# Two heads per strip in the value product, and an output chain that runs once per two batches

## What is computed

```python
def _mha(x, ctx, mask, qw, qb, kw, kb, vw, vb):          # H = 16 heads, D = 128
    q = _split_heads(x @ qw + qb); k = _split_heads(ctx @ kw + kb); v = _split_heads(ctx @ vw + vb)
    scores = jnp.einsum('bqhd,bkhd->bhqk', q, k) / np.sqrt(D // H) (+ mask)
    probs = jax.nn.softmax(scores, axis=-1)
    return jnp.einsum('bhqk,bkhd->bqhd', probs, v).reshape(...)
def _self_output(h, residual, w, b, g, be):
    h = h @ w + b + residual
    return (h - mean) * rsqrt(var + 1e-05) * g + be
ca = _mha(x, ctx, mask, cq.., ck.., cv..);  x = _self_output(ca, x, co_w, co_b, co_g, co_be)
sa = _mha(x, x, None, sq.., sk.., sv..);    x = _self_output(sa, x, so_w, so_b, so_g, so_be)
inter = gelu(x @ fi_w + fi_b);              x = _self_output(inter, x, fo_w, fo_b, fo_g, fo_be)
```

## Time and profile before

| | |
|---|---|
| median of 3 runs | 1085.51 us (1085.27 to 1091.91) |
| span of the profiled execution | 1077.5 us |
| PE busy | 966.2 us (90%) |
| PE weight loads | 747.5 us (69%) |
| DVE busy | 642.9 us (60%) |
| ACT busy | 571.7 us (53%) |
| POOL busy | 468.3 us (43%) |
| exponentials of the 128 chunks, starts | 35.0 to 432.3 us |
| mean granted TensorE clock | 0.975 of full speed |

### The profile page before, as it was taken

How to read it: one execution, slowest core, us unless ns; L and a number is a source line. 1 busy time by engine, 2 the same in 40 slices (tenths; PEclk the granted TensorE clock), 3 DMA queues, 4 the chain that set the end, 5 groups by cost and what they waited for, 6 DMA issues and landing times. The chain is left out here.

```text
span 1077.5 us, 23011 instructions
## 1 busy us (share of the span) xinstructions
PE 966.2 (90%) x8722; PEld 747.5 (69%) x8726; DVE 642.9 (60%) x2007; ACT 571.7 (53%) x1209; POOL 468.3 (43%) x752
## 2 busy tenths in 40 slices
PE   4889998998999799988989999888888999999998
PEld 2556666565656566777877887766667777778787
DVE  3657777677778564665763333446888457466241
ACT  4768887777676465423334332123333845755553
POOL 6246675758686744665520000233445244213010
PEclk9989999999999899999999999989999999999999
DMA  7756443323332120000002331300000331521421
GB/s 179 188 137 163 114 122 80 85 72 105 84 99 70 41 84 7 15 12 6 6 26 67 108 108 54 111 20 15 20 21 11 92 100 25 94 80 40 138 65 53
DMA packets 72942, 78.56 MB, mean 73 GB/s; under 512 B 8469, under 2 KB 64132, under 8 KB 72832
## 3 DMA queue, kind: packets, MB, share of 16 engines
q1 hardware_dynamic: 67104, 69.61, 23.2%
q0 software_dynamic: 4096, 6.84, 3.0%
q10 hardware_dynamic: 1632, 0.64, 0.3%
HBM read 38.25 MB, written 11.68 MB: 46 GB/s over the span
## 5 line engine op out<-in xcount | busy, mean ns | idle before, releaser
L1286 DVE TENSOR_REDUCE arena<-pb 128x8 f32<-128x1024 f32 (+1 forms) x128 | 128.4, 1007 | 60.0 <-PE pb L647 56.5
L1780 ACT ACTIVATE arena<-pb 128x1024 f32<-128x1024 f32 (+1 forms) x128 | 130.8, 1022 | 58.9 <-PE pb L663 51.0
L2292 POOL DMA_INDIRECT arena<-yd,arena x64 | 63.9, 999 | 141.4 <-issue 141.3
L1834 ACT ACTIVATE arena<-pb 128x256 f32<-128x256 f32 x128 | 48.0, 383 | 131.0 <-PE pb L832 103.6
L831 PE MATMUL pb<-XLT,arena 128*128 128x256 f32 x256 | 80.2, 396 | 10.0 <-DVE arena L1445 7.5
L680 PE MATMUL pb<-arena 77*32 77x128 f32 (+1 forms) x2048 | 85.1, 285 | 0.0
L2171 POOL DMA_INDIRECT xd<-XB,arena x64 | 64.0, 1000 | 33.1 <-issue 19.2
L832 PE MATMUL pb<-XLT,arena 128*128 128x256 f32 x256 | 78.0, 387 | 0.0
L2030 ACT ACTIVATE arena<-pb,arena 128x264 f32<-128x264 f32 x128 | 54.7, 482 | 37.4 <-PE pb L1135 37.3
L2088 POOL TENSOR_SCALAR arena<-arena 128x4 f32<-128x4 f32 x48 | 9.4, 196 | 147.2 <-DVE arena L1241 144.8
L1441 DVE SCALAR_TENSOR_TENSOR arena<-arena,pb 128x256 f32<-128x256 f32 x128 | 53.0, 414 | 25.5 <-ACT arena L1834 19.7
(11 more groups left out here) (233 smaller groups left out, 2386.1 us busy)
## 6 DMA issues: line engine op xcount, KB each, us to landing
arena<-arena SPq DMA_DIRECT2D x190, 128.0 KB, 2.4
arena<-in_pe SPq DMA_DIRECT2D x32, 514.5 KB, 3.7
arena<-in_pr SPq DMA_DIRECT2D x8, 768.0 KB, 5.0
arena<-arena SPq DMA_DIRECT2D x43, 77.0 KB, 2.2
xd<-arena SPq DMA_DIRECT2D x8, 320.0 KB, 3.0
arena<-xd SPq DMA_DIRECT2D x8, 320.0 KB, 5.7
yd<-arena SPq DMA_DIRECT2D x8, 320.0 KB, 5.2
XO<-in_x SPq DMA_DIRECT2D x8, 256.0 KB, 3.2
```

What stands on the lines that cost most here:

```text
L1286: e.tensor_reduce(NM[i % 2][0][:, b, 4 * h:4 * h + 4, :].rearrange("p t h -> p h t"), sc, AX, ALU.max, negate=True).then_inc(v_max, 1)
L1780: e.activation(PT[n % 2][0:nk, :], bk2[1][0:nk, :], ACT.Exp, scale=SC8).then_inc(a_exp, 1)
L2292: e.indirect_dma_start(G[x % 8], None, yd, bass.IndirectOffsetOnAxis(ap=IDG.bitcast(U32)[:, k, b:b + 1], axis=0), bounds_check=None, oob_i ...
```

## The change

V gets 18 columns a head (eight of V, one of ones, nine of zeros), in two tiles of its own (`VA`) instead of in the three sets. The two heads of a pair now share a strip: the first head's weights are its 18 columns and what follows; the second's begin nine columns ahead of its own, so that its nine land in places 9 to 17 of the strip, and its matmul accumulates onto the first. A bank then holds two batches, and the chain behind it runs once per pair of batches: `out_sums`, `ttr`, `on`, `to`, `ont`, `two`, `tw` at beats 4, 5, 6, 6, 6, 7, 8 and four beats later for the second pair, with one buffer of each tile instead of two. With only two `VA` tiles, `values` moves from beat -14 to -8 and `va` from -13 to -7, and values get a semaphore of their own.

The bias of V is added in `ont`'s copy (a bias column instead of a plain copy). so_b and fo_b are added once to the shift rows of the layer norm ahead (`join_rows` on POOL), and taken off again in the copies of the turned groups (`turned_less`), so the eight additions for s units and the eight for the feed-forward go; for c units POOL still adds co_b. The four small products at the start go.

```diff
@@ pe @@
-                if h == 0:
+                if j % 4 == 0:
                     L.wait_ge(a_va, i + 1)
                     L.wait_ge(*free[4])
-                    free[4] = (a_os, 4 * i + b + 1)
+                    free[4] = (a_os, 2 * i + b // 2 + 1)
                 L.wait_ge(a_exp, n + 1)
-                for q in (2 * h, 2 * h + 1):
+                c = 128 * (2 * (b % 2) + h)
+                for half in range(2):
                     for k in range(4):
-                        h9, t, h2 = 144 * b + 9 * (4 * q + k), 2 * (q - 2 * h) + k // 2, k % 2
-                        ins = e.matmul(bk[4][32 * k:32 * k + 32, 128 * q:128 * q + 128], va[0:nk, h9:h9 + 32],
-                                       PT[n % 2][0:nk, 512 * h2 + 128 * t:512 * h2 + 128 * t + 128],
-                                       start=True, stop=True)
+                        v0 = VW * (NH * b + 8 * h + 2 * k + half) - 9 * half
+                        p0 = 512 * half + 128 * k
+                        ins = e.matmul(bk[4][32 * k:32 * k + 32, c:c + 128], va[0:nk, v0:v0 + 32],
+                                       PT[n % 2][0:nk, p0:p0 + 128], start=(half == 0), stop=(half == 1))
...
-                for i in at(n, -14, "c", lo=2):
-                    values(i)
-                for i in at(n, -14, "s", lo=2):
+                for i in at(n, -8, lo=2):
                     values(i)
@@ act @@
-                e.activation(OS[x % 2], bk[4], ACT.Copy).then_inc(a_os, 1)
+                e.activation(OS, bk[4], ACT.Copy).then_inc(a_os, 1)
...
-                L.wait_ge(p_kqv, 3 * i + 3)
+                L.wait_ge(p_val, i + 1)
                 L.wait_ge(g_vo, 1)
-                if i >= 3:
-                    L.wait_ge(p_pv, 8 * (i - 2))
+                if i >= 2:
+                    L.wait_ge(p_pv, 8 * (i - 1))
...
+            def turned_less(g, j, ready, done):
+
+                L.wait_ge(v_neg, 1)
+                L.wait_ge(*ready)
+                e.activation(xlt(g), bk[5], ACT.Identity, bias=NEGB[:, j:j + 1]).then_inc(done, 1)
...
-                e.activation(ONT[x % 2], bk[7][:, 0:128], ACT.Copy).then_inc(a_ont, 1)
+                e.activation(ONT, bk[7][:, 0:256], ACT.Identity, bias=vb[:, j:j + 1]).then_inc(a_ont, 1)
...
-                for i in at(n, -13, lo=2):
+                for i in at(n, -7, lo=2):
                     va(i)
@@ dve @@
+                L.tick(e.reciprocal(RC, v4[:, :, :, 8]))
+                L.own_done()
+                e.tensor_tensor(ON.rearrange("p (s h d) -> p s h d", h=2, d=8), v4[:, :, :, 0:8],
+                                RC.unsqueeze(3).to_broadcast([128, 16, 2, 8]), ALU.mult).then_inc(v_on, 1)
...
+                e.tensor_tensor(x2, bk[7][:, 0:256], x2, ALU.add).then_inc(v_tw, 1)
@@ pool @@
+            def join_rows():
+
+                L.wait_ge(d_rows, 32)
+                L.tick(e.tensor_tensor(R_["co_be"], R_["co_be"], R_["so_b"], ALU.add))
+                L.tick(e.tensor_tensor(R_["so_be"], R_["so_be"], R_["fo_b"], ALU.add))
...
-            def bias_ffn(g):
-                L.front_done()
-                L.wait_ge(p_tf, g + 1)
-                e.tensor_tensor(grp(XB, g), grp(XB, g), bcast(R_["fo_b"], GB), ALU.add).then_inc(g_fb, 1)
-                L.in_front(g_fb, g + 1)
...
-                for i in at(n, 2, "s"):
                     bias_out(i)
```

More of the change, by code:

```diff
@@ L95 @@
 NU = len(UNITS)
+VW = 18
 NCH = 8 * NU
@@ L134, in at, with pair_at @@
     return [i] if r == 0 and lo <= i < hi and UNITS[i][0] in kinds else []
-def block_at(n, d, kinds="cs"):
-    return [(i, b) for b in range(4) for i in at(n, d + 2 * b, kinds)]
+def pair_at(n, d, kinds="cs"):
+    return [(i, p) for p in range(2) for i in at(n, d + 4 * p, kinds)]
 def chunk_at(n, d):
@@ L373, in program @@
                 ("SC", (128, 512)), ("TG", (128, 512)))})
-        EWP = [rl(128, 1029) for _ in range(3)]
+        EWP = [rl(128, 1029) for _ in range(2)]
         XE, YT = r(128, 8, N8), r(128, 8, N8)
-        EWP.append(r(128, 1029))
+        EWP += [r(128, 1029) for _ in range(2)]
         OHP += [(r(128, 8, CAP2), r(128, 8, CAP2))]
@@ L755, in ttr, with to, two @@
                 for q in range(4):
-                    ins = e.transpose(bat(bk[5], q), OS[x % 2][:, 128 * q:128 * q + 128], ident)
+                    ins = e.transpose(bat(bk[5], q), bat(OS, q), ident)
                 ins.then_inc(p_ttr, 1)
                 free[5] = (v_on, x + 1)
-            def to(i, b):
-                x = 4 * i + b
+            def to(i, p):
+                x = 2 * i + p
                 L.wait_ge(v_on, x + 1)
                 L.wait_ge(*free[7])
-                e.transpose(bk[7][:, 0:128], ON[x % 2][1], ident).then_inc(p_to, 1)
+                for b in range(2):
+                    ins = e.transpose(bat(bk[7], b), bat(ON, b), ident)
+                ins.then_inc(p_to, 1)
                 free[7] = (a_ont, x + 1)
-            def two(i, b):
-                x = 4 * i + b
+            def two(i, p):
+                x = 2 * i + p
                 L.wait_ge(a_ont, x + 1)
                 L.wait_ge(*free[7])
-                e.matmul(bk[7][:, 0:128], ONT[x % 2], W[UNITS[i][0] + "o"], start=True, stop=True).then_inc(p_two, 1)
+                for b in range(2):
+                    ins = e.matmul(bat(bk[7], b), bat(ONT, b), W[UNITS[i][0] + "o"], start=True, stop=True)
+                ins.then_inc(p_two, 1)
                 free[7] = (v_tw, x + 1)
@@ L2129, in pool @@
             e.memset(mhalf, -0.5)
-            for s in range(3):
-                ins = e.memset(SETS[s][2], 1.0)
+            for s in range(2):
+                ins = e.memset(VA[s], 0.0)
+            L.tick(ins)
+            L.own_done()
+            for s in range(2):
+                ins = e.memset(VA[s][:, 0:GB * NH * VW].rearrange("p (h d) -> p h d", d=VW)[:, :, 8:9], 1.0)
             ins.then_inc(g_vo, 1)
```

234 lines of the change are left out of this document (92 added, 142 removed).

## The result

The changed kernel takes 1101.87 us (median of 17 runs, 1092.06 to 1110.55); the kernel before, run beside it, 1086.46. The ratio is 1.0111, 95% interval 1.0082 to 1.0140. Two repeats beside the experiments gave 1.0132 (1.0091 to 1.0173) and 1.0092 (1.0058 to 1.0126). So it is slower by about 12 us, just at the 1% that I had called measurable. (The two medians are 15.4 us apart; the ratio leaves out two of the 17 executions of the changed kernel, which fell into a slower state.) My forecast was +5 us. 1101.9 lies inside the range of 1072 to 1103, at its upper edge, but outside the 1080 to 1098 that the replay itself had claimed; the 12 us of the ratio, put onto the 1085.51 it started from, would be 1097.5, just inside that too.

What follows compares the result with a forecast made beforehand. The chain of second score product and exponential was taken to pace the quiet units, though TensorE looks full. Terms 6.5 + 5 - 2 - 3.5 - 1 = +5 gave 1077.5 + 5 + 8.0 = 1090.5 us, range 1072 to 1103.

Steps and rivals of the forecast that it cites:

- The replay of a quiet unit: Unit 3 beat by beat: values wait for ScalarE's query copies, beat 0 takes 4.55 us, unit +1.3; units 1 to 5 +6.5.
- The spread chain: Beat 5's first s1 waits for spread query operands (ScalarE, POOL, DMA), 1.65 us later, swallowing the 0.6 gained in beats 3 and 4.
- All of it shifts with s1, so the gains of beats 1 to 3 are swallowed: Units 7, 9, 11, 13: beat 0 +1.6, VectorE, POOL and ScalarE work behind s1 shifts too; 4 x 1.3 = +5 us.
- units 6, 8, 10 and 12: Values cost only +1.0 in beat 0, later beats give 0.7, 0.5 and 0.3: 4 x -0.5 = -2 us.
- rival B: New gaps in beats 0 and 5 pull TensorE's clock down; nine dips of 1.5 us make 1104 us; 18%.
- because VectorE waits in these beats: VectorE's strided reads in the attention beats: from nothing to some 10 us, taken as hidden and left unpriced.
- Head and tail: Head -1 us (unit 2's values leave unit 0, small bias products go); tail, units 14, 15 and after, -3.5 us (fewer transposes).
- 8.0 us lie around the span: Profiled span 1077.5 us against the runs' median 1085.51; 8.0 us added to the forecast span.
- POOL's relief: Eight plus eight bias additions removed from POOL, some 20 us, counted at nothing because POOL is waited for behind L1248.
- The bias column: ScalarE copies with a bias column cost at least 0.05 us more each, 2 us over 48 copies, mostly hidden.
- A: Freed time comes through on all engines: 1065 us, or about 1075 with half of the waits left; 22%.
- C: In the value product the second head's matmul waits for the first in its strip: 35 us, 1125 us; 2%.

Runs made afterwards that it cites:

- e1: Changed kernel with the value projection and its copy two beats later, so no longer behind fresh queries on bank 6: 1071.97 us, ratio 0.9937.
- e2: Kernel before with only the move of values and their copy, with a semaphore of their own; no packing, pairs or folded biases: 1100.47 us, ratio 1.0218.
- e3: Changed kernel with the value projection in the same place but written to bank 7, so without the wait: 1071.69 us, ratio 0.9930; again 1068.20 us, 0.9886.
- e6: e3 with 16 unread additions of 128x480 put back on POOL where the bias additions had stood: 1088.12 us, ratio 0.9999.
- e7: e3 with two transfers of the queries' middle part put ahead of the wait for POOL's low part in SyncE's queue: 1084.20 us, ratio 0.9964.
- e5: e3 with 32 unread blocks of four transposes put back on TensorE, in beats 3 and 7 of every unit: 1093.98 us, ratio 1.0069.
- e9: e3 with 32 unread copies of 128x480 put back on ScalarE behind the exponentials of beats 2 and 6: 1075.22 us, ratio 0.9960.
- e8: Changed kernel with five unread filling matmuls ahead of each value projection in beat 0 only: 1089.97 us, ratio 1.0088.
- e4: Changed kernel with unread filling matmuls, five ahead of each value projection (beat 0), three ahead of each unit's first score product (beat 5): 1088.47 us, ratio 1.0101.

## Why the prediction came out as it did

**The replay of a quiet unit was right.** Beat by beat in unit 3, forecast and found: 4.55 and 4.70, 1.95 and 1.78, 1.85 and 1.85, 1.56 and 1.77, 1.56 and 1.66; beats 5 to 7 together 7.8 and 7.4; the unit 19.2 and 19.1. The mechanism is shown from both sides by e1, e2 and e3: values behind fresh queries on one bank wait for ScalarE, and s1 and s2 wait behind them. Units 1 to 5 come to +6.8 for +6.5, though not unit by unit: unit 2 has 20.9 us for 18.2 in the two executions in which its clock was 0.92, and 19.5 in the one at full clock.

**The spread chain** as what swallows the gain of beats 3 and 4 was half right. The s1 of beat 5 does wait for the DMA, but e3, e6 and e7 together show a second chain, VectorE's, as late as that one, and e5 shows that 0.4 us added in beat 3 come out at the end of the unit. So beats 3 and 4 have little slack after all, and the gain I gave them (0.6) was to be had only where TensorE itself ended the beat. From the weight loads' 12.03 of 18.00 us I had concluded that little of TensorE's relief need come through; of the 19.6 us that e5 puts back about three quarters did.

**"All of it shifts with s1, so the gains of beats 1 to 3 are swallowed" (units 7, 9, 11, 13)** has the right sign, +7.0 for +5, but in part by luck: unit 7 gives only +0.3 of its 1.3, and 5.5 come from units 9 and 11, where the clock differs (below).

**The term that missed** is that of units 6, 8, 10 and 12, -2 forecast, +2.8 found. "Values cost only +1.0" was right where nothing else is late (units 6 and 8: -0.3 and -0.4 for -0.5 each). Units 10 and 12 differ from one execution of the same kernel to the next by up to 4.4 us. Length in us and, in brackets, the granted clock of that stretch:

| unit | before | changed, its three profiled executions |
|---|---|---|
| 9 | 24.5 (0.93) | 27.0 (0.81), 27.1 (0.81), 25.7 (0.87) |
| 10 | 28.7 (1.00) | 33.2 (0.85), 29.0 (1.00), 30.0 (1.00) |
| 11 | 24.8 (0.93) | 26.6 (0.94), 31.5 (0.84), 27.9 (0.94) |
| 12 | 29.2 (1.00) | 28.6 (1.00), 31.4 (0.89), 33.0 (0.90) |

At full clock unit 10 is 0.3 and 1.3 us above the kernel before and unit 12 0.6 below it; the three long ones stand at a lower clock. So what the sum lacks here goes with the lower clock, the symptom of rival B, which my sum had put at nothing; that the clock is the cause of the length is argued, not shown. I had also priced the pairs' VectorE work at nothing "because VectorE waits in these beats". It waits before the score product and is wanted right behind it: in the third execution `to` waits 4.11 us for it in unit 12, and the clock falls at the end of that wait. But in the other two no wait of `to` in units 10 and 12 reaches 0.5 us, so this is not what makes them long.

**Head and tail** were given -1 and -3.5 and came out at +2.8 and -0.5. For the head the baseline is the fault: the one profiled execution of before was a lucky one. From its start to the first exponential the clock was 1.00; in the profiles of all other kernels it was 0.75 to 0.85 there, in e2 too, whose head is nearly that of before. Its span plus the 2 us that lie around it (1105.39 - 1103.3 in the changed kernel's) make 1079.6, 6 us under the median; "8.0 us lie around the span" was wrong, 6 of them were this. The tail's term is not decided: e2, in which nothing of the tail is changed, has 713.1 for 712.9, but the three executions of the changed kernel spread from 707.8 to 716.8, and e1 and e3 have 704 to 708.

**POOL's relief "at nothing"** was mis-sized: 5 to 8 us with some 4 of uncertainty (e6), at a place that I don't know. **The bias column** was right in kind: L1785 with it takes 0.47 us where a plain 256-wide copy, L1800, takes 0.38, and L1778 0.69 where L1767, 512 wide and plain, takes 0.60: 0.09 us each, where I had at least 0.05. The Trainium skill (ScalarE: Activation LUTs, section What ACT_TABLE_LOAD costs) gives some 93 ns for each pointer operand, such as a bias column, which these rows bear out.

**The rivals.** A needed beat 0 near 3 us and fell; but with the wait gone (e1, e3) the kernel is 7 to 12 us faster than before, the half of A that I had called 1075. It is not 20 although e5, e6 and e9 price the three reliefs at 13 to 16, 5 to 8 and 7 us: such prices need not add up, and the pairs bring costs of their own, which no kernel measures alone. B has its symptom, a mean clock of 0.953 for 0.963, worth 5 to 10 us by the spread of the runs, and that is as large as what my sum lacks (12 - 5); e3's mean clock of 0.957 suggests that part of it went with the wait. Its mechanism, dips brought by the beat-0 gap alone, fell with e2 and e8; B had named the gap in beat 5 as well, and that half is open (e4). So +12 us stands between the forecast's +5 and B's +18.5: the replay was right about the wait, and that the stated range holds 1101.9 is owed to its having been widened towards B. How the missing 7 us divide between clock, pairs and noise I can't say. C fell: the sixteen passes of a value block take 0.64 us as before, two heads in a strip or not.

## What to carry to other kernels

When an operation moves, ask first which bank or buffer it writes and whose copy empties that: here some 20 us hung on one bank number, and the order of all instructions could stay. A relief of an engine is worth what it is worth in the beats that this engine ends; measure it by putting dummy work back where the old work stood, and expect the values of several engines not to add up. Before reading a difference of single microseconds between two profiles, compare the granted clock stretch by stretch: here the start-up of the kernel before had run at full clock in its one profile, and in none of the other 13. The version to keep is e3_bank7 (ratios 0.9930 and 0.9886), which beats both kernels; e1_beat2 (0.9937) is as good.
